# Moving the rotary angles, a weight pre-sum and a residual add to other places in a twelve-layer decoder kernel

## The reference, cut to what matters

```python
def _L2_ffn_ref(x, w_r, b_r, w1, b1, w2, b2):          # the half-token layer
    scores = jnp.einsum('bld,d->bl', x, w_r) + b_r
    _, idx = jax.lax.top_k(scores, k)                   # half of each sequence's tokens
    h = jax.nn.gelu(jnp.einsum('bkd,df->bkf', x_sel, w1) + b1)
    out_sel = jnp.einsum('bkf,fd->bkd', h, w2) + b2     # the other tokens get 0

def _L3_attn_ref(x, W_in, W_out, gamma, beta, D):       # 32 heads, a scan over 256 steps
    ...
    y = jnp.moveaxis(ys, 0, 1).reshape(Bz, Lz, D_INNER) # D_INNER = 2048
    y = y * jax.nn.silu(z_t)
    mu, var = y.mean(-1, keepdims=True), y.var(-1, keepdims=True)
    y = (y - mu) * jax.lax.rsqrt(var + EPS) * gamma + beta
    return y @ W_out.T
```

## Time and profile before

| what | value |
|---|---|
| median of 3 runs | 2460.75 us (2460.51 to 2464.7) |
| the profiled execution's own time | 2457.14 us |
| its span, first to last instruction | 2455.1 us |
| busy: PE / DVE / ACT / POOL | 1993.3 (81%) / 1757.1 (72%) / 1346.2 (55%) / 422.0 (17%) us |
| mean granted TensorE clock | 0.862 |
| half-token stage, in the trace | 1595.1 to about 1667.8 us |
| `l3s` | about 1681 to 1698.3 us |
| heads and `l3c`, four sequences | 1698.3 to about 2135.7 us |
| `l3e` | 2135.7 to about 2160.1 us |

### The profile page before, as it was taken

How to read it: one execution, slowest core, us unless ns; L and a number is a source line. 1 busy time by engine, 2 the same in 40 slices (tenths; PEclk the granted TensorE clock), 3 DMA queues, 4 the chain that set the end, 5 groups by cost and what they waited for, 6 DMA issues and landing times. The chain is left out here.

```text
span 2455.1 us, 34758 instructions
## 1 busy us (share of the span) xinstructions
PE 1993.3 (81%) x11337; PEld 1308.3 (53%) x11337; DVE 1757.1 (72%) x3886; ACT 1346.2 (55%) x2636; POOL 422.0 (17%) x585
## 2 busy tenths in 40 slices
PE   6999999987767775856866896496999999958978
PEld 4777776764333333634654353364766666733545
DVE  6878788767999998755786874665737364568734
ACT  5877777766898986354334265523333333352641
POOL 2333333312111101004531000201101010110000
PEclk7999999997777777786787698598999999986989
DMA  5000000003111103204202100050000000042010
GB/s 220 3 2 3 2 4 1 1 1 117 39 59 58 39 1 97 83 5 95 45 7 66 58 3 19 22 226 2 1 2 0 2 0 2 1 110 74 16 37 18
DMA packets 61982, 94.52 MB, mean 39 GB/s; under 512 B 9387, under 2 KB 48123, under 8 KB 59367
## 3 DMA queue, kind: packets, MB, share of 16 engines
q1 hardware_dynamic: 58556, 87.81, 11.5%
q0 software_dynamic: 1728, 4.22, 0.7%
q10 hardware_dynamic: 1536, 0.49, 0.1%
HBM read 80.53 MB, written 10.49 MB: 37 GB/s over the span
## 5 line engine op out<-in xcount | busy, mean ns | idle before, releaser
L1260 DVE SCALAR_TENSOR_TENSOR moe_acc<-moee_eo,moe_wsel,moe_acc 128x256 f32<-128x256 bf16 x512 | 226.7, 514 | 0.6
L867 DVE SCALAR_TENSOR_TENSOR l_acc<-l_px,l0w_chan,l_acc 128x253 f32<-128x253 f32 (+2 forms) x288 | 137.6, 478 | 79.9 <-POOL l_acc L835 79.4
L1192 ACT CAST moee_eo<-moee_po 128x512 bf16<-128x512 f32 x256 | 132.6, 597 | 38.4 <-PE moee_po L1165 35.6
L1165 PE MATMUL moee_po<-moee_db,moee_hb 96*128 96x256 bf16 (+1 forms) x768 | 131.1, 336 | 22.4 <-ACT moee_eo L1192 13.6
L1150 PE MATMUL moee_pu<-moe_xb,moee_wb 128*128 128x512 bf16 x192 | 73.7, 525 | 83.7 <-DVE moee_ub L1249 83.7
L1165 PEld LDWEIGHTS moee_po<-moee_db,moee_hb 96*128 96x128 bf16 (+1 forms) x768 | 89.3, 118 | 71.5 <-ACT moee_eo L1192 19.1
L1704 ACT ACTIVATE l3xa_ex<-l3xa_pS 128x512 f32<-128x512 f32 x128 | 74.1, 605 | 80.6 <-PE l3xa_pS L1617 76.2
L351 PE MATMUL ln_pt<-ident,xn 128*128 128x128 f32 x176 | 39.8, 418 | 95.7 <-DVE xn L277 95.7
L1704 ACT ACTIVATE l2a_ex<-l2a_pS 128x512 f32<-128x512 f32 x128 | 73.8, 605 | 76.8 <-PE l2a_pS L1617 72.2
L540 PE MATMUL l_pz<-xT,l0w_w_in 128*128 128x256 f32 x384 | 111.4, 413 | 2.5 <-DVE l_sz L915 2.5
L540 PE MATMUL l_px<-xT,l0w_w_in 128*128 128x256 f32 x384 | 103.5, 393 | 4.3 <-DVE l_acc L867 4.3
(11 more groups left out here) (616 smaller groups left out, 5503.5 us busy)
## 6 DMA issues: line engine op xcount, KB each, us to landing
moe_wf<-in_moe_up SPq DMA_DIRECT2D x48, 256.0 KB, 3.0
l3w_w_in<-in_l_w_in SPq DMA_DIRECT2D x1, 8224.0 KB, 25.4
m1b_bc<-bc_rows SPq DMA_DIRECT2D x16, 512.0 KB, 10.8
moe_df<-in_moe_down SPq DMA_DIRECT2D x48, 128.0 KB, 3.3
l_qs<-parts_q SPq DMA_DIRECT2D x36, 128.0 KB
l0w_w_in<-in_l_w_in SPq DMA_DIRECT2D x2, 1536.0 KB, 12.9
l0w_w_out<-in_l_w_out SPq DMA_DIRECT2D x1, 3072.0 KB
parts_q<-l_pieces SPq DMA_DIRECT2D x16, 192.0 KB, 2.3
```

The source lines that it names most:

```text
L867: nc.vector.scalar_tensor_tensor(out=a, in0=px[:, 0:S - (L0_CONV - 1 - c)], scalar=w, in1=a, op0=ALU.mult, op1=ALU.add).then_inc(tap_done, 1)
L1165: last = nc.tensor.matmul(po[:, t, :], hb[rows, j % H, t * P:(t + 1) * P], db[rows, j % H, :], start=(n == 0), stop=(n == len(parts) - 1))
L1192: nc.scalar.copy(eo[:, e % 2, 2 * q:2 * q + 2, :], po[:, 2 * q:2 * q + 2, :]).then_inc(o_read, 1)
L1260: last = nc.vector.scalar_tensor_tensor(out=acc[:, t, :], in0=eo[:, e % 2, t, :], scalar=wsel[:, t, e:e + 1], in1=acc[:, t, :], op0=ALU.mu ...
```

## The change

It has four parts.

1. In the half-token stage, the positions are loaded ahead of the wait for the scores, and `axial_angles` stands before the counting instead of after it.
2. `scale_and_sum` takes one slice with each of the 8 output tiles instead of two. The other 8 slices stand in `l3s` behind `split_rows`, and TensorE's product of the sums, which waits for them, stands behind `px` instead of before it.
3. In `mamba3_ends` with an end, `gw[1]` is added to `res` while TensorE still makes `po`; the first of the three instructions per tile moves ahead of the wait for ScalarE's guess; and the last two become one that writes `res`.
4. ScalarE asks for the table set that holds both Ln and Exp before it waits for the variance.

The diff, with renames, unchanged bodies and the declaration of the semaphore `sums_done` left out:

```diff
@@ half_tokens @@
                     sp.dma_start(b2[:, :], I["l2f_b2"]).then_inc(second_in, 16)
+                    sp.dma_start(ang[:, :], I["l3x_pos"]).then_inc(pos_in, 16)
+                    sp.dma_start(meta[:, :], I["l3x_meta"]).then_inc(pos_in, 16)
                     sp.wait_ge(score_row, 1)
...
                     sp.dma_start(row[:, :], g["score_row"].broadcast_to([P, TOK])).then_inc(row_in, 16)
-                    sp.dma_start(ang[:, :], I["l3x_pos"]).then_inc(pos_in, 16)
-                    sp.dma_start(meta[:, :], I["l3x_meta"]).then_inc(pos_in, 16)
...
                     nc.vector.tensor_copy(by_tile[:, :], po[0:NT, 0, 0:P]).then_inc(score_row, 1)
+                    axial_angles(nc, dve, link, rope, ang, turns, meta, pos_in, angle)
                     dve.wait_ge(score_done, 1)
                     dve.wait_ge(row_in, 16)
...
-                    axial_angles(nc, dve, link, rope, ang, turns, meta, pos_in, angle)
                     dve.wait_ge(second_in, 32)
                     for t in range(NT):
-                        for j in range(t * L3_J // NT, (t + 1) * L3_J // NT):
-                            scale_and_sum(dve, link, j)
+                        if t == 0:
+                            dve.wait_ge(ahead["out_in"], 32)
+                        scale_and_sum(nc, link, ahead, t)
                         dve.wait_ge(down, t + 1)
@@ mamba3_ends, tensor @@
-                if end is None:
-                    for n in range(2):
-                        last = nc.tensor.matmul(po[:, n, 0:D], g["ones"][:, 0:P], m["sums"][:, n, :], ...)
-                    last.then_inc(gw_ready, 1)
                 if start is not None:
                     for n in range(ST * NQ):
...
+                if end is None:
+                    pe.wait_ge(sums_done, 1)
+                    for n in range(2):
+                        last = nc.tensor.matmul(po[:, n, 0:D], g["ones"][:, 0:P], m["sums"][:, n, :], ...)
+                    last.then_inc(gw_ready, 1)
@@ mamba3_ends, scalar @@
                 if end is not None:
+                    nc.scalar.preload_act_table_set(EXP_LN)
                     act.wait_ge(var_ready, 1)
@@ mamba3_ends, vector @@
                 if end is not None:
+                    for t in range(ST):
+                        now = res4(res)[:, end, t, :]
+                        link(nc.vector.tensor_tensor(now, now, gw[:, 1, :], ALU.add))
                     dve.wait_ge(used, ST)
...
+                    link(nc.vector.tensor_scalar(small[:, 7, :], small[:, 0, :], -1.0, None, ALU.mult))
+                    for t in range(ST):
+                        last = nc.vector.scalar_tensor_tensor(out=tmp[:, t, :], in0=gw[:, 0, :],
+                                                              scalar=small[:, 7, t:t + 1], in1=po[:, t, 0:D],
+                                                              op0=ALU.mult, op1=ALU.add)
+                    link(last)
                     dve.wait_ge(guess, 1)
                     newton_rsqrt(nc, link, small[:, 5, :], small[:, 3, :], small[:, 6, :])
-                    link(nc.vector.tensor_scalar(small[:, 7, :], small[:, 0, :], -1.0, None, ALU.mult))
                     for t in range(ST):
-                        link(... L3194 ...)
-                        link(... L3197 ...)
-                        nc.vector.tensor_tensor(res4(res)[:, end, t, :], res4(res)[:, end, t, :], tmp[:, t, :], ALU.add)
+                        now = res4(res)[:, end, t, :]
+                        nc.vector.scalar_tensor_tensor(out=now, in0=tmp[:, t, :], scalar=small[:, 5, t:t + 1], in1=now,
+                                                       op0=ALU.mult, op1=ALU.add)
                 if end is None:
+                    for j in range(NT, L3_J - 1):
+                        scale_and_sum(nc, link, m, j)
+                    ... the slice L3_J - 1 in the same three instructions, the last with .then_inc(sums_done, 1)
                     dve.wait_ge(gw_ready, 1)
                     nc.vector.tensor_copy(gw[:, :, :], po[:, :, 0:D])
```

More of the change, by code:

```diff
@@ L2243, with scale_and_sum @@
 MOD_KEEP = S // 2
+def scale_and_sum(nc, link, m, j):
+    w_out, sums, gamma, beta = m["w_out"], m["sums"], m["chan"][:, j, 1:2], m["chan"][:, j, 2:3]
+    row = w_out[:, j, 0:D]
+    if j == 0:
+        nc.vector.memset(w_out[:, :, D:D + 1], 1.0)
+        link(nc.vector.tensor_scalar(sums[:, 1, :], row, beta, None, ALU.mult))
+        link(nc.vector.tensor_scalar(row, row, gamma, None, ALU.mult))
+        return
+    link(nc.vector.scalar_tensor_tensor(out=sums[:, 1, :], in0=row, scalar=beta, in1=sums[:, 1, :],
+                                        op0=ALU.mult, op1=ALU.add))
+    link(nc.vector.tensor_scalar(row, row, gamma, None, ALU.mult))
+    before = w_out[:, 0, 0:D] if j == 1 else sums[:, 0, :]
+    link(nc.vector.tensor_tensor(sums[:, 0, :], before, row, ALU.add))
 def half_tokens(nc, g, ahead):
@@ L2273, in half_tokens @@
             rope = g["xn"][:, :, :].rearrange("p (n t) d -> p n (t d)", n=2)
-            w_out, chan, sums = ahead["w_out"], ahead["chan"], ahead["sums"]
+            w_out, chan = ahead["w_out"], ahead["chan"]
             ph = st.psum("ph", [P, 4, 512])
@@ L2281, in half_tokens @@
             pos_in, angle, sine, tables_out, second_in = st.sem("pos_in", "angle", "sine", "tables_out", "second_in")
-            def scale_and_sum(dve, link, j):
-                gamma, beta = chan[:, j, 1:2], chan[:, j, 2:3]
-                row = w_out[:, j, 0:D]
-                if j == 0:
-                    dve.wait_ge(ahead["out_in"], 32)
-                    nc.vector.memset(w_out[:, :, D:D + 1], 1.0)
-                    link(nc.vector.tensor_scalar(sums[:, 1, :], row, beta, None, ALU.mult))
-                    link(nc.vector.tensor_scalar(row, row, gamma, None, ALU.mult))
-                    return
-                link(nc.vector.scalar_tensor_tensor(out=sums[:, 1, :], in0=row, scalar=beta, in1=sums[:, 1, :],
-                                                    op0=ALU.mult, op1=ALU.add))
-                link(nc.vector.tensor_scalar(row, row, gamma, None, ALU.mult))
-                before = w_out[:, 0, 0:D] if j == 1 else sums[:, 0, :]
-                link(nc.vector.tensor_tensor(sums[:, 0, :], before, row, ALU.add))
             with st.block() as block:
@@ L3114, in mamba3_ends @@
         (x_in, a_proj, a_exp, v_chain, split_done, rows, proj, taken, used, var_ready, a_chain, guess, scaled,
-         gw_ready) = st.sem(
+         gw_ready, sums_done) = st.sem(
             "x_in", "a_proj", "a_exp", "v_chain", "split_done", "rows", "proj", "taken", "used", "var_ready",
-            "a_chain", "guess", "scaled", "gw_ready")
+            "a_chain", "guess", "scaled", "gw_ready", "sums_done")
         with st.block() as block:
@@ L3140, in _ @@
                                          start=True, stop=True).then_inc(used, 1)
-                if end is None:
-                    for n in range(2):
-                        last = nc.tensor.matmul(po[:, n, 0:D], g["ones"][:, 0:P], m["sums"][:, n, :], start=True,
-                                                stop=True)
-                    last.then_inc(gw_ready, 1)
                 if start is not None:
@@ L3155, in _ @@
                         last.then_inc(proj, 1)
+                if end is None:
+                    pe.wait_ge(sums_done, 1)
+                    for n in range(2):
+                        last = nc.tensor.matmul(po[:, n, 0:D], g["ones"][:, 0:P], m["sums"][:, n, :], start=True,
+                                                stop=True)
+                    last.then_inc(gw_ready, 1)
             @block.scalar
```

12 lines of the change are left out of this document (6 added, 6 removed).

## The result

The changed kernel took 2448.16 us (median of 10 runs, 2442.12 to 2453.06), the kernel before 2460.63 beside it (10 runs). The ratio is 0.9950 [0.9938, 0.9963], so it is 12.3 us faster, between 9.1 and 15.3 (the two medians are 12.5 apart). The forecast was 8.9 us: 2451.9, in a range of 2447.5 to 2457.0. The median lies in that range, but outside the narrower one of 2449.5 to 2454.5 that the forecast gave its own mechanism. The profiled span is 2444.2 us against 2455.1.

The account below looks back on a forecast made before the run. It took VectorE to bound the half-token stage, TensorE `l3s` and `l3c`, and the serial tail behind the variance `l3e`. Terms -7.4 + 0.9 - 2.7 + 0.3 = -8.9 took 2460.75 to 2451.9 us, range 2447.5 to 2457.0.

Parts of the forecast that it names:

- its own mechanism: Whole kernel: all terms come out as forecast, 2451.9 us within 2449.5 to 2454.5; chance 0.70.
- The half-token stage: Half-token output tiles: VectorE no longer holds TensorE up, so the stage ends 7.4 us earlier, bounds 6.6 and 7.6.
- TensorE's unstalled end: Half-token stage: without waits for VectorE, TensorE's matmuls end some 0.8 us earlier, at 1658.3 instead of 1659.06.
- `l3s`: First block of the tenth layer: eight slices and the sums' product behind `px` cost 0.8 to 0.9 us.
- The tail of `l3e`: From the variance to the last `res`: reordering, one instruction less and no table load between Ln and Exp gain 2.7 us.
- The moved loads: First step of the four heads stages: a table load before Tanh costs 0 to 0.1 us each, 0.3 in all.
- both rivals that rested on two loads' price: Heads stages: each moved table load costs two loads' time, giving 2457.0 or 2462.4 us; chances 0.14 and 0.03.
- the first of them: Heads stages: a load at two loads' time costs 1.35 us each, 5.4 in all, giving 2457.0; chance 0.14.
- the second, with 2.71 kept in each stage: Heads stages: the double-priced load's delay is never made up, 10.8 us in all, giving 2462.4; chance 0.03.
- `l3c`: The `l3c` stages: TensorE sets the pace, so the residual, reordering and table set are worth nothing there.
- The late angles: Half-token stage: positions land late, so VectorE is late at the first tile, giving 2454; chance 0.04.
- the rival in which `l3c` gains: Three `l3c` stages: ScalarE's 1.28 us load held `px`, so they give 3.9 us more, 2448.0; chance 0.09.

Follow-up runs that it names:

- k1: Kernel before with only the angles and the positions' DMAs moved ahead of the counting; ratio 0.9983, 4.2 us faster.
- k10: Kernel before with only one slice per output tile and the other eight slices in `l3s`; 2449.73 us in a single execution.
- k4: Changed kernel run again without any edit; ratio 0.9963 to the kernel before, 9.1 us faster.
- k3: Kernel before with only the changed ends of the tenth layer and the early table set; ratio 1.0002, no change.
- k5: Changed kernel with two slices per tile and the product of the sums where it was before; ratio 0.9975, 6.2 us faster than the kernel before.
- k8: Changed kernel with one more table load before the first Tanh of each heads stage; ratio 0.9979 to the kernel before.
- k11: Kernel before run once more without any edit; ratio 1.0008, medians 2462.70 and 2459.47 us.
- k2: Changed kernel with the angles and positions' DMAs back where they were in the kernel before; ratio 0.9972, 6.9 us faster than the kernel before.
- k6: Changed kernel with 14 slices in the half-token layer, two in `l3s`, and the product of the sums amid `px`; ratio 0.9953 to the kernel before.
- k7: Changed kernel without the early request for the table set with Ln and Exp; 2452.5 us in a single execution.
- k9: Changed kernel with the Tanh table set asked for at the head of each heads stage; 2454.09 us in a single execution.
- k12: Changed kernel with unread TensorE products behind `po` in `l3e` and at the start of two normalizations; ratio 0.9954 to the kernel before.

## Why the prediction was right, and where it was not

**The half-token stage: right in mechanism, a little too much.** Forecast -7.4, measured 30.16 - 37.14 = -6.98. The mis-sized term is TensorE's unstalled end. The forecast took a tile at 3.42 and 0.8 us of recovery. The 3.42 and 3.60 of the earlier trace rows are the widths of the two windows, not the measured time of a tile. The 3.60 is borne out by VectorE's rows (1640.47, 1644.07, 1647.67 in the trace before). The 3.42 is a little short: VectorE's rows after the change stand 3.45 apart (1634.72 to 1655.42 in six tiles), TensorE's 128 matmuls take 27.89, and the recovery is 28.36 - 27.89 = 0.47. What it did not say is that the two parts do the same work: alone, part 1 brings 5.9 (k1) and part 2 brings 7.0 (k10).

**`l3s`: right at full clock.** Forecast +0.8 to 0.9 with a short wait of TensorE, measured +0.82 with a wait of 0.45 (k4). In the trace of the changed kernel itself the stage is 1.81 longer, and 1.0 of that is the lower clock in `px`, which k1, k3 and k5 show without the slices. Why TensorE's clock is low there in eight of fourteen executions stays open: the normalization ahead of it took the same to within 0.2 us.

**The tail of `l3e`: right.** Forecast -2.7, measured -2.92 for the stretch that it spoke of: 2.08 from the order and the merged instruction, 0.84 from the table set. The two tiles' last instructions take 0.88 together, where 0.48 + 0.4 was reckoned, and the four of Newton 0.8.

**The moved loads: right.** Forecast 0 to 0.1 a stage, measured 0.03. Tanh starts 20 ns behind the load, and k8's two loads in a row start 1.29 us apart, with Tanh 10 ns behind the second. The Trainium skill, "ScalarE: Activation LUTs", section "What ACT_TABLE_LOAD costs", counts a drain of 1380 ns beside the load; no trace here shows it, at the old place or at the new. The measurement decides: one load is 1.28 us here, and both rivals that rested on two loads' price fall with it. k8 shows at the same time what the first of them was worth: 1.30 a stage, once and not at every step, where it had reckoned 1.35. Its price was right and its condition wrong; the second, with 2.71 kept in each stage, had the price wrong too.

**`l3c`: right.** In all kernels its three stages take 99.4 to 101.5 in sum, with the order of before and with the new one. A single stage takes between 32.7 and 34.2, in kernels of both kinds. The table set gains nothing there.

**The late angles: excluded.** VectorE's first row of them stands at 1606.30, right behind `by_tile`.

**What the sum did not contain: the normalization and the projections behind `l3e`.** The forecast added its terms as if what follows took the same time. It doesn't: this is a term that the sum put at nothing without a reason. The eleventh layer's projections, from the first `l3xp` product to the first `l3xa` product, take:

```
ends as before:  before 42.35  k1 42.04  k10 43.48  k11 41.50               mean 42.3
ends changed:    after 44.58  k2 44.31  k3 45.07  k5 45.95  k6 44.51
                 k7 45.28  k8 44.08  k9 45.28  k4 42.23  k12 43.81          mean 44.5
```

The window that begins with the first of them, in the trace before and after:

```profile
2169.60:2173.20 3.60, 3.60 (x9) 1.69 (x10) 0.00 (x0) 3.60 (x2) 0.52 (x1) 1.00 0.63 208
```

```profile
2156.37:2159.97 3.60, 3.60 (x5) 1.53 (x6) 0.00 (x0) 3.60 (x2) 0.52 (x1) 0.50 0.64 209
```

The clock is 1.00 in the one and 0.50, the lower level, in the other, and TensorE starts 9 matmuls against 5. The low start comes in 8 of 10 executions with changed ends and in none of four without. It is not that TensorE had been idle longer: ahead of the transposes it was idle for 9.24 us after the change, and for 12.38 before. That the shorter tail brings the low start on is argued from these counts; the one kernel that was to act on this clock is k12, which started at 1.00, but so did k4, the changed kernel again, without its products.

What a low start costs can be read from VectorE, which sets the pace of the projections from its second unit on (before, then after):

```profile
2174.82 0.69 DVE L1439 TENSOR_TENSOR l3xp_t<-l3xp_pm,l3xr_rope 128x512 f32<-128x512 f32 x1 [6.02 <-DMA l3xr_rope<-rope_tables]
...
2177.17 0.69 DVE L1439 TENSOR_TENSOR l3xp_t<-l3xp_pm,l3xr_rope 128x512 f32<-128x512 f32 x1 [0.20 <-PE l3xp_pw L1354]
```

```profile
2162.04 0.69 DVE L1439 TENSOR_TENSOR l3xp_t<-l3xp_pm,l3xr_rope 128x512 f32<-128x512 f32 x1 [6.47 <-PE l3xp_pw L1354]
...
2165.83 0.69 DVE L1439 TENSOR_TENSOR l3xp_t<-l3xp_pm,l3xr_rope 128x512 f32<-128x512 f32 x1 [1.64 <-PE l3xp_pw L1354]
```

Its second unit begins 7.57 us behind the first projection before, and 9.46 after, where it waits 1.64 us for TensorE. The third unit follows 3.85 us later in both, so the delay is carried on as it stands. Its last row ends 36.65 to 36.76 us behind the first projection in the five executions with a full-clock start other than k12, and 38.33 to 38.80 in the eight with a low one: 1.9 us. The normalization ahead, with its transposes, adds some 0.25 (9.37 to 9.41 us against 9.11 to 9.27). What follows VectorE's last row takes 4.8 to 7.2 us in both groups and is scatter; that is why k10, at full clock, has 43.48. k12 removes the low start and wins little of this, since the DMA of the rotation tables, which VectorE's first product waits for whenever the start is at full clock, came 1.6 us later there.

`l3e` and *rest* together average 319.05 us in the four executions and 317.9 in the ten. Of about 3.3 us that `l3e` gives in the mean (24.67 to 21.38), 1.2 come through to the end, and 2.7 where the projections still started at full clock (k4 and k12: 316.4). The single sums scatter by more than this difference, 318.2 to 320.4 in the four and 316.0 to 319.3 in the ten, and k8 has 316.6 with a low start; the 1.9 us of VectorE's rows are the firmer figure. That the clock costs this time is shown; what sets it from one execution to the next is not.

**The sum from the stretches** is then -7.0 in the half-token stage, +0.1 or +0.8 in `l3s`, +0.1 in the heads, and -1.2 to -2.7 in `l3e` and behind it: between -7.3 and -9.5. The second measurement, -9.1 [-11.6, -6.4], holds it and the forecast of -8.9. The first, -12.3 [-15.3, -9.1], reaches only the far end of the sum and just leaves the forecast out; in its trace 3.3 of the 10.9 us of span lie in *lead*, where the change has done nothing yet but for its last tens of us. I count the surplus over -9 as scatter of that kind; the repeat supports that, and no experiment isolates it. So it is the mechanism, stretch by stretch, that was right. That the number came so close is in part luck: the loss behind `l3e` was left out of the sum, and the two measurements, -12.3 and -9.1, stand further apart than that loss. The first median, 2448.16, stands next to the 2448.0 of the rival in which `l3c` gains, which the traces exclude. No other version is shown to beat the changed kernel: k6 and k12 lie within its interval.

## What to carry to other kernels

When two edits remove the same lateness, work out each alone as well as both: a late start with spare pace behind it and a slow pace with an early start cost nearly the same, and mending one makes the other nearly free. A serial tail that is cut in front of TensorE work moves that work in time, and here the clock there was mostly lower afterwards, so read the granted clock of the stretch behind it before the gain is booked. And a table load costs nothing only as long as what waits for it has slack for all of it (here one load fits and a second costs its full 1.30); where a preload is asked for, look at where the other loads of the loop went.

## What was not expected of the hardware

The level of TensorE's clock at the same place differs between executions of one kernel: the first 3.3 us of `px` in `l3s` ran at 0.56 in one execution of the changed kernel and at 1.00 in another, and `px` took 15.70 and 14.00 us. So two profiles of one kernel differ, in one stage, by more than what an edit there costs.

A shorter idle time did not give a higher clock. With 9.24 us of TensorE's idle time ahead of the transposes the projections started at 0.50 in one execution of the changed kernel and at 1.00 in another; with 12.38 us, in the kernel before, at 1.00.

Two table loads back to back take twice 1.28 us, with 10 ns between them and 10 ns to Tanh; one hidden load costs 0.03 us in its stage, the second one 1.30, the full length.
